# Expert results by indirect DMA on one Trainium2 core: adding into rows of the output, or writing each result to a row of its own and summing afterwards

## The reference, cut to what matters

```python
logits = xf @ router_w.T                       # xf: the 4096 normalised tokens
k_probs, k_idx = top_k(softmax(logits), 2)     # two different experts per token
k_probs = k_probs / sum(k_probs)
rank = place of the pair in its expert's queue # capacity 1281 pairs per expert
keep = rank < capacity
h = silu(buf @ w1); out_buf = h @ w2           # per expert: 128 -> 512 -> 128
combined = sum over the token's two pairs of k_prob * out_buf row (0 if not kept)
result = combined + xf + x1                    # x1: the residual after the attention
```

## Time and profile before

| what | us |
|---|---|
| median of 3 runs | 521.02 |
| the profiled execution, its own time | 516.97 |
| its span, first to last instruction | 515.0 |
| POOL busy with L1486 (80 instructions) | 129.0 |
| POOL busy with L1406 (64 instructions) | 100.8 |

### The profile page before, as it was taken

The page is one execution under the profiler, slowest core; times in us unless marked ns, Lnnn a source line. Parts: engine busy times, 40 slices in busy tenths (PEclk is TensorE's granted clock), DMA queues, the critical chain, the costliest instruction groups (busy, mean ns, idle before and its releaser), DMA issues.

```text
span 515.0 us, 16333 instructions
## 1 busy us (share of the span) xinstructions
PE 409.9 (80%) x5659; PEld 322.7 (63%) x5659; DVE 361.2 (70%) x1138; ACT 261.9 (51%) x587; POOL 322.9 (63%) x250
## 2 busy tenths in 40 slices
PE   3553598989999999999999953889989999989500
PEld 2342466767777777777777742478877877877400
DVE  4786367787988989888888763077778678777300
ACT  1111254555555665555665632198868768768000
POOL 7442023175777767777665587207688888888882
PEclk9997789998999999999999995999999999999855
DMA  8986876777788887888988445535565565543331
GB/s 190 235 206 172 219 196 154 200 181 162 180 183 180 196 195 170 184 184 184 208 184 167 67 44 83 114 98 111 84 123 76 85 130 74 86 38 36 36 35 12
DMA packets 89046, 70.32 MB, mean 137 GB/s; under 512 B 8992, under 2 KB 75808, under 8 KB 88480
## 3 DMA queue, kind: packets, MB, share of 16 engines
q1 hardware_dynamic: 68208, 60.09, 45.8%
q0 software_dynamic: 20784, 9.53, 19.9%
HBM read 38.85 MB, written 30.74 MB: 135 GB/s over the span
## 4 chain that ended last, share of the span: by engine, by line
SPq 25%; PE 24%; DMA 15%; issue 14%; POOL 10%; ACT 7%; DVE 4%; DVEq 0%; POOLq 0%; ACTq 0%
PE bank L479 20%; DMA k_scratch<-parts 6%; SPq L378 5%; DMA k_pack<-k_scratch 5%; SPq L376 5%; SPq L358 4%; POOL queues L1406 4%; POOL out L1486 4%; SPq L363 4%; ACT hidp L918 3%; ACT hid L914 3%; DMA q_pack<-maxT 2%; PE bank L703 2%; SPq L388 2%; DMA queues<-rows,index 1%
## 5 line engine op out<-in xcount | busy, mean ns | idle before, releaser
L1486 POOL DMA_INDIRECT out<-ys,row_token x80 | 129.0, 1613 | 50.0 <-issue 47.0
L943 DVE TENSOR_REDUCE maxima<-bank 128x4 f32<-128x512 f32 x128 | 87.7, 687 | 35.5 <-PE bank L479 31.6
L1406 POOL DMA_INDIRECT queues<-rows,index x64 | 100.8, 1576 | 18.0 <-issue 17.7
L806 ACT ACTIVATE probs<-bank 128x512 f32<-128x512 f32 x128 | 76.4, 597 | 54.6 <-PE bank L479 54.1
L1354 DVE TENSOR_TENSOR hidp<-hid,hidp 128x512 fp32r<-128x512 f32 (+1 forms) x96 | 57.2, 604 | 25.7 <-ACT hidp L918 24.5
L479 PE MATMUL bank<-k_pack,q_pack 128*64 128x128 bf16 x1024 | 55.1, 233 | 15.7 <-DMA k_pack<-k_scratch 15.1
L479 PE MATMUL bank<-q_pack,k_pack 128*128 128x64 bf16 x1024 | 53.1, 196 | 14.8 <-DMA q_pack<-maxT 14.3
L479 PE MATMUL bank<-xTp,w1p 128*128 128x512 f32 (+1 forms) x288 | 61.1, 361 | 2.8 <-DVE xTp L1216 2.8
L479 PE MATMUL bank<-hidp,w2p 128*128 128x512 f32 (+1 forms) x288 | 62.2, 365 | 0.0
L479 PE MATMUL bank<-probs,v_sb 128*32 128x64 f32 x2048 | 56.0, 226 | 5.7 <-ACT csb L813 3.0
L914 ACT ACTIVATE hid<-bank 128x512 f32<-128x512 f32 (+1 forms) x96 | 54.2, 564 | 10.1 <-PE bank L479 9.9
(11 more groups left out here) (148 smaller groups left out, 691.1 us busy)
## 6 DMA issues: line engine op xcount, KB each, us to landing
k_pack<-k_scratch SPq DMA_DIRECT2D x64, 192.0 KB, 3.8
q_pack<-q_scratch SPq DMA_DIRECT2D x64, 128.0 KB, 3.1
queues<-empty SPq DMA_DIRECT2D x8, 682.5 KB, 7.6
xs<-queues SPq DMA_DIRECT2D x7, 650.0 KB
q_scratch<-parts SPq DMA_DIRECT2D x16, 192.0 KB
k_scratch<-parts SPq DMA_DIRECT2D x16, 192.0 KB
xin<-in_x SPq DMA_DIRECT2D x16, 128.0 KB, 3.1
cin<-in_ctx SPq DMA_DIRECT2D x16, 128.0 KB
```

The costliest lines, as they stand in the source:

```text
L806: nc.scalar.activation(probs[u % 2][:], bb[u % 2][:], ACT.Exp).then_inc(S["prob_s"], 1)
L943: v.reduce_max(maxima[par][:, 4 * hg:4 * hg + 4, i2], ab[u % 2][:].rearrange("p (h c) -> p h c", c=P), AX).then_inc(S["max_s"], 1)
L1406: g.indirect_dma_start(queues, bass.IndirectOffsetOnAxis(ap=index[par][:, n:n + 1], axis=0), rows[par][:, n // TILES, n % TILES, :], None, ...
L1486: g.indirect_dma_start(out, bass.IndirectOffsetOnAxis(ap=row_token[par][0:n, t:t + 1], axis=0), ys[c][0:n, col // P, :], None, compute_op= ...
```

## The change

The DRAM tensor `results` gets a row of its own for each of a token's two expert results: rows 0 to 4095 for the expert with the lower number, rows 4096 to 8191 for the higher one, and dump rows behind. The tag now carries that row's number. The results are written there by indirect DMAs without an add, and so are the queue rows. Nothing meets any more, so all of `find_meetings`, `add_meetings`, `meeting_rows`, `left_tags` and `left_results` goes, and the waits of POOL on earlier adds with them; the 4 places of tile 10 are written by an indirect DMA per expert (11 per expert). `base` stays in SBUF for all 16 batches and is no longer stored to `out`. SP zeroes `results` (4 MB, 8 DMAs of 64 partitions by 8 KB) in rounds 14 to 17 of stage 1. After experts 0 to 6 have landed, SP reads the lower rows back (4 DMAs of 512 KB, "early") and DVE adds them to `base`; after expert 7 has landed, it reads the higher rows (8 DMAs of 256 KB, "late"), DVE adds `base` to each piece and SP stores each piece to `out`. In the diff, calls are cut short; the functions that are dropped, and PE's waits on `found` and `met`, are not shown in it. `tags` loses one cast.

```diff
+    results = nc.dram_tensor("results", [PLACES + QUEUE, DIM], F32).ap()
-        base = two("base", [P, TILES, DIM])
+        base = sb("base", [P, BATCHES, TILES, DIM])
...
@@ SP, start @@
-            sp.dma_start(out[ALL:ALL + QUEUE, :].rearrange("(p r) c -> p r c", p=INIT_P),
-                         empty[:, :, 0:DIM]).then_inc(S["dump_out"], 16)
@@ SP, body @@
-                if on(k - 2):
-                    after(sp, "base_s", 1, k - 2)
-                    sp.dma_start(out[bass.ds((k - 2) * TOKENS, TOKENS), :]...,
-                                 base[par][:]).then_inc(S[f"base_out{par}"], 16)
...
+                if isinstance(k, int) and k >= BATCHES - 2:
+                    for n in range(2 * (k - BATCHES + 2), 2 * (k - BATCHES + 3)):
+                        sp.dma_start(results[n * CLEAR:(n + 1) * CLEAR, :]..., empty...
+                                     ).then_inc(S["results_clear"], 16)
@@ SP, after the batches @@
-            for e in range(EXPERTS):
-                sp.dma_start(left[TAIL * e:TAIL * (e + 1), :], queues[...]).then_inc(S["left_in"], 16)
...
+            added_all(sp, EXPERTS - 1)
+            for n in range(BATCHES // QUARTER):
+                sp.dma_start(early[:, n * QUARTER:(n + 1) * QUARTER, :, :]..., results[at:at + QUARTER * TOKENS, :]...)
             added_all(sp, EXPERTS)
+            for n in range(pieces):
+                sp.dma_start(late[n][:], results[ALL + ...]).then_inc(S[f"late_in{n}"], 16)
+            for n in range(pieces):
+                sp.wait_ge(S["summed"], n + 1)
+                sp.dma_start(out[at:at + PIECE * TOKENS, :]..., late[n][:]).then_inc(S["out_written"], 16)
@@ PE, results_across @@
-                for t, col, n in full_tiles(c):
+                for t, col, n in tiles_of(c):
@@ DVE, normalise_result @@
-                    after_same(dve, "base_out", 16, par, pair, -4)
@@ DVE, base_and_tags @@
-                v.tensor_tensor(rows[par][:, :, :, DIM + 1], rows[par][:, :, :, DIM + 1], tag_step[:], ALU.add)
+                v.tensor_tensor(tok[par][:], tok[par][:], tag_step[:], ALU.add).then_inc(S["tok_step"], 1)
@@ DVE, route, n = 2 and n = 3 @@
+                    v.tensor_tensor(later[:], top_index[:, :, 0], top_index[:, :, 1], ALU.is_gt)
+                    v.scalar_tensor_tensor(rows[par][:, :, :, DIM + 1], later[:]..., float(ALL), tok[par][:], ALU.mult, ALU.add)
@@ DVE, weigh_results @@
+                for t, col, n in tiles_of(c):
+                    if n < P:
+                        v.tensor_scalar(ys[c][0:n, col // P, :], yt[0:n, col:col + DIM], row_gate[...], None, ALU.mult)
@@ DVE, after the experts @@
+            for n in range(BATCHES // QUARTER):
+                v.tensor_tensor(here, here, early[:, n * QUARTER:(n + 1) * QUARTER, :, :], ALU.add)
+            for n in range(BATCHES // PIECE):
+                v.tensor_tensor(late[n][:], late[n][:], base[:, PIECE * n:PIECE * (n + 1), :, :]..., ALU.add)
@@ POOL, rows_out @@
-                                         rows[par][...], None, compute_op=ALU.add).then_inc(S[f"scattered{par}"], 16)
+                                         rows[par][...], None).then_inc(S[f"scattered{par}"], 16)
@@ POOL, before the experts @@
-                pool.wait_ge(S[f"base_out{n}"], 16 * BATCHES // 2)
+            pool.wait_ge(S["results_clear"], 16 * PLACES // CLEAR)
@@ POOL, body2 @@
-                        pool.wait_ge(S["paired"], 3 * (e - 1))
...
-                        added_all(pool, e)
...
-                    for t, col, n in full_tiles(c):
-                        g.indirect_dma_start(out, ..., ys[c][0:n, col // P, :], None, compute_op=ALU.add)
+                    for t, col, n in tiles_of(c):
+                        g.indirect_dma_start(results, ..., ys[c][0:n, col // P, :], None)
@@ POOL, after the experts @@
-            pool.wait_ge(S["left_ready"], 1)
-            g.indirect_dma_start(out, ..., left_ys[:, 1, :], None, compute_op=ALU.add)
```

More of the change, by code:

```diff
@@ L127, in build @@
         tag_step = sb("tag_step", [P, 2, TILES])
+        tok = two("tok", [P, 2, TILES])
+        later = sb("later", [P, TILES])
         half_neg = sb("half_neg", [P, TILES])
@@ L196, in build @@
         yT = two("yT", [P, 512])
-        ys = [sb(f"ys{c}", [P, len(full_tiles(c)), DIM]) for c in range(NCH)]
+        ys = [sb(f"ys{c}", [P, len(tiles_of(c)), DIM]) for c in range(NCH)]
         with ExitStack() as packs:
@@ L1091, in route @@
                     after(dve, "indexed", 2, j)
+                    after(dve, "tok_s", 1, j - 1)
+                    apart(dve, "past_dve")
+                    v.tensor_tensor(later[:], top_index[:, :, 0], top_index[:, :, 1], ALU.is_gt).then_inc(S["later_s"], 1)
                     done(v.tensor_tensor(chosen[:],
@@ L1099, in route @@
                     v.tensor_tensor(both16[:], chosen[:, 0, :, :], chosen[:, 1, :, :], ALU.add).then_inc(S["both_s"], 1)
+                    after(dve, "later_s", 1, j)
+                    apart(dve, "past_dve")
+                    after(dve, "tok_step", 1, j)
+                    v.scalar_tensor_tensor(rows[par][:, :, :, DIM + 1], later[:].unsqueeze(1).to_broadcast([P, 2, TILES]),
+                                           float(ALL), tok[par][:], ALU.mult, ALU.add).then_inc(S["tok_s"], 1)
                 elif n == 4:
@@ L1374, in _ @@
             weigh_results(e, e % 2, NCH - 1, s)
-            left_results()
+            for n in range(BATCHES // QUARTER):
+                dve.wait_ge(S[f"early_in{n}"], 16)
+                here = base[:, n * QUARTER:(n + 1) * QUARTER, :, :]
+                v.tensor_tensor(here, here, early[:, n * QUARTER:(n + 1) * QUARTER, :, :], ALU.add
+                                ).then_inc(S["early_sum"], 1)
+            for n in range(BATCHES // PIECE):
+                dve.wait_ge(S["early_sum"], n * PIECE // QUARTER + 1)
+                dve.wait_ge(S[f"late_in{n}"], 16)
+                v.tensor_tensor(late[n][:], late[n][:],
+                                base[:, PIECE * n:PIECE * (n + 1), :, :].rearrange("p b t c -> p (b t) c"), ALU.add
+                                ).then_inc(S["summed"], 1)
         @block.gpsimd
```

201 lines of the change are left out of this document (52 added, 149 removed).

## The result

The changed kernel takes 501.70 us, the median of 4 runs (495.69 to 503.06); beside it the kernel before took 521.9. The ratio is 0.9585, 95% interval 0.9537 to 0.9632: faster. The forecast was 510. The profiled execution took 502.08 us, its span is 500.2.

A forecast was written before the change was run, and what follows sets the result against it. PE was taken to bound stage 1, POOL's indirect issues stage 2. With PE pacing stage 2, its last issue at 477.2 plus 30.3 for the end and -3 for stage 1 gave span 504.5, median 510 us, range 500 to 543.

The forecast's parts named there:

- The price: POOL's time for an indirect DMA without an add: 1.03 us, two thirds of the 1.54 with an add.
- Stage 2: Expert stage: POOL needs 15.3 us per expert, under PE's 16.35, so PE sets the pace; expert 7 starts at 446.7.
- Stage 1: Batch rounds before the experts: four terms sum to -3 us, bounds -13 to +13.
- The base store's -4: SP's rounds in stage 1: without the 16 base stores, 0.4 us saved in each of ten rounds, 8 at most.
- the DVE steps' +1: Stage 1: two more small DVE instructions per batch, taken as +1 us, between 0 and +5.
- the last scatters' -3: End of stage 1: four issues shorter by 0.51 us and a shorter wait for POOL, -3; bounds 0 and -5.
- The zeroing: Late stage 1: zeroing `results` makes batch 15's maxima land late and shares the DMA engines, +3 us; bounds 0 and +8.
- The end: Last issue to span's end: landing 3.0, SP 0.3, reading back 22, carried-over 5.0, together 30.3 us against 7.7 before.
- The cover: Loads and sums of the early half lie under expert 7; up to 10 us more if that is gone.
- POOL stays the bound: Rival, stage 2: at 1.41 us per issue POOL sets the pace, median 536; 549 at an unchanged 1.54. Chance 0.30.
- the end or the zeroing cost more: Rival: PE-paced, but reading back takes 30 us and stage 1 loses 4; 525, no change. Chance 0.15.
- More comes back: Rival: SP's loop gains its 8 us and reading back overlaps to 16; median 500. Chance 0.08.

The follow-up runs named there:

- run 1: The changed kernel with the add back in the indirect DMAs of the expert results alone: 533.46 us, ratio to the kernel before 1.021.
- run 6: The changed kernel with DVE's four sums of the early half moved behind the landing of expert 7: 497.69 us, ratio 0.9565.
- run 2: The changed kernel with the add back in the indirect DMAs of the queue rows alone: 504.18 us, ratio 0.966.
- run 3: The changed kernel with SP's store of the base rows to the output back in each round: 506.78 us, ratio 0.9706.
- run 4: The changed kernel with the eight zeroing DMAs of results moved behind the loads of expert 1: 495.86 us, ratio 0.9482.
- run 10: The changed kernel with 6 instead of 10 placeholder products on PE ahead of expert 0: 497.76 us, ratio 0.9585.
- run 5: The changed kernel with the same zeroing at the same place, written as rows of 512 bytes instead of 8 KB: 496.91 us, ratio 0.9541.
- run 8: The changed kernel with a wait at POOL's end for the landing of the last store to the output: 505.6 us, ratio 0.9714.
- run 7: The changed kernel with the early half's loads issued only when expert 7 has landed too: 504.04 us, ratio 0.9672.

## Why the prediction was right, and where not

**The price: right.** 1.03 was taken, 0.96 came, and run 1 shows that the sign hangs on it: at 1.56 the change loses 2%. The reason given for it holds less well. Between 4 and 128 rows a plain issue grows by (0.960 - 0.885)/124 = 0.6 ns a row, one with an add by (1.556 - 1.341)/124 = 1.7 ns. So of the 0.6 us that the add costs, 0.46 do not depend on the rows at all, and "two thirds, by the lists" hit the value by luck, through a proportion that the rows don't bear out. The Trainium skill's two read descriptors per chunk ("Collectives: The Full Stack", section "The bandwidth ceiling: the fold count and why AG ≠ RS ≠ AR") would have given 0.77 by length of the list; the measured 0.96 is above it.

**Stage 2: right in kind.** PE-paced throughout. From expert 0 to expert 7 it takes 115.40 us (334.35 to 449.75) where 7 x 16.35 = 114.45 were forecast: +1.0. Most of that was in the rows already: the step from expert 0 to 1 is the short one in both kernels (16.17 before, 16.11 after) and the next is 16.50 before and 16.55 after, so the mean of the two was too low for the other six. What the tile of 4 rows adds can be little more than those 0.05 per expert; no run separates it.

**Expert 7's issues: a missing term.** The sum had them at 1.33 each, beside idle engines. DVE's early sums, called hidden, cost POOL 2.0 us through its last issues (run 6). The Trainium skill ("GPSIMD Engine Reference", section "1. Specifications") says that POOL's interfaces to SBUF are shared with DVE, with contention beside DVE instructions that have two SBUF inputs; the trace agrees with 0.96 stretched to as much as 1.68 under a sum of two SBUF tiles, and shows besides that the issue has to begin inside the sum.

**Stage 1: the sum failed, -3 forecast and +2.1 found.** The base store's -4 and the DVE steps' +1 came as -3.8 by batch 10 together and -2.9 by batch 14, and the last scatters' -3 as -3.5 (their last issue is 0.5 earlier than before although batch 15 was 3.0 later). Which edit gave the -3.8 is open in part: run 2 leaves little of it to the adds, and run 3 doesn't settle the store. The 0.81 that the store's slot was read as is 1.03 in the rows (200.44 to 201.47), so its bound was 10 and not 8. Two terms failed. The zeroing was put at +3 by way of the maxima of batch 15; these were in time, and instead DVE's wait for the scatters of batch 12 ended 9.2 us after the last of them was begun, and batch 15 went from 2.9 early to 3.0 late: 5.9, of which run 4 gives back 5.5 (13.9 to 8.5 between the milestones of batches 14 and 15). And the placeholder products, which stand in the code and in the trace, were not in the sum: in the kernel before they ended 0.7 before the rows came, here 3.6 behind them (run 10). The rule of the Trainium skill ("DMA: Bandwidth & Descriptors", section "Queues, rings and completion order") foretold the late scatters; my reading of it, one row of zeros in front of each scatter row, fell with run 5. By that page a packet typically holds 9 to 17 descriptors, which would make the length of one row matter less; the profile counts one packet for each row of zeros (run 5), so no run here shows how many an engine takes in one turn.

**The end: two terms too long.** 30.3 us forecast, 500.2 - 481.57 = 18.6 found. The reading back was put at 22 with 230 GB/s; from the first late load (483.62) to the end of the span it takes 16.6, and the page gives 277 GB/s in the last slice, nearer to the bound of 14. The 5.0 "carried over" were no property of the end but of POOL ending late (run 8), and here SP ends last. Landing took 2.0 instead of 3.0; the 1.8 that the prediction calls the least landing of the adds belongs to SP's stores into the same tensor, and the adds alone have 2.7/3.3/4.9. The cover, priced at up to 10, is 7 (run 7).

Together: 504.5 + 5.1 (stage 1) + 1.0 (pace) + 1.3 (expert 7's issues: +2.0 for the sums, -0.7 for the price) - 11.7 (end) = 500.2, which is the span. That the forecast of the span was only 4.3 us off is thus luck in part: errors of +7.4 and -11.7 stand in it. The other half of the miss in the median, 4.4 of 8.8, is the 4.05 us carried over from the kernel before, whose profiled execution lay below its median; that of the changed kernel lies 0.4 above.

**The rivals.** "POOL stays the bound" is run 1. Of "the end or the zeroing cost more" the zeroing did, by 3, and the end did the opposite. "More comes back" named 500, and by the right mechanism for a half of it: the reading back at 16, with 16.6 found.

## What to carry to other kernels

An add in an indirect DMA has a price on the issuing engine, and where that engine paces a stage, writing to rows of one's own and summing later can pay although it moves more bytes. When a stage ends earlier or later, look for what was timed to the old moment: placeholder work, zeroing, loads queued behind it. Price work called hidden by what it shares with its neighbours, and bulk transfers by who else is waiting for a landing just then.

## What was not expected of the hardware

- A plain indirect issue is nearly flat in rows: 0.89 us for 4, 0.96 for 128. An issue of 128 rows with the add has 112 packets more than a plain one in the pages of runs 1 and 2 alike (13824 and 12032 in the software queue, against 4864 in the changed kernel).
- An indirect issue that begins inside a DVE instruction with two SBUF operands is longer by what is left of that instruction, less some 0.13 us; one that begins before it, or within 0.03 us of its start (418.75 us of the changed kernel), is not.
- Zeros of 4.2 MB in flight delayed the landing of scatters, counted from the start of a batch's last issue to the end of DVE's wait: 3.4 us in the kernel before, 9.2 beside zeros in rows of 8 KB, 8.5 beside rows of 512 bytes.
- About 5 us follow POOL's last work when POOL is the last to finish, and none show when SP is.
- A placeholder pass took 0.85 us while the granted clock was 0.50 (1.2 GHz, 322 to 326 us of the changed kernel) and 0.43 at 1.00 (2.4 GHz, from 328), so the same twenty lasted 11.71 us there and 10.30 in run 5, where the clock was 1.00 from 324 on.
